# Cross attention of a decoder block: the Q and K projections as seven block products instead of eight

## The reference

```python
def _L0_xattn_ref(hidden_states, key_value_states, attention_mask, position_bias, ln_weight, w_q, w_k, w_v, w_out):
    ...
    x = _rmsnorm(hidden_states, ln_weight)
    ...
    h_q = (x @ w_q.T).reshape(b, lq, H, DH)
    h_k = (key_value_states @ w_k.T).reshape(b, lk, H, DH)
    h_v = (key_value_states @ w_v.T).reshape(b, lk, H, DH)
    score = jnp.einsum('bqhd,bkhd->bhqk', h_q, h_k)
    score = score + position_bias[None]
    m = attention_mask[:, None]
    score = jnp.where(m, score, -jnp.inf)
    score = jax.nn.softmax(score, axis=-1)
    score = jnp.where(m, score, 0.0)
    attn = jnp.einsum('bhqk,bkhd->bqhd', score, h_v).reshape(b, lq, H * DH)
    out = attn @ w_out.T
    return hidden_states + out
```

## Time and profile before

| what | us |
|---|---|
| median of 3 runs | 1096.17 |
| the profiled execution's own time | 1095.16 |
| its span, first to last instruction | 1093.1 |
| TensorE busy | 1061.4 (97%) |
| VectorE busy | 559.0 (51%) |
| ScalarE busy | 517.1 (47%) |
| GpSimd busy | 253.9 (23%) |
| one group of the cross attention, 297.47 to 350.92 | 53.45 |

### The profile page before, as it was taken

One profiled execution on the slowest core, in us unless ns is written; L12 is line 12 of the kernel. 1 busy time (PEld: TensorE's weight loads), 2 busy tenths in 40 slices (PEclk: granted clock), 3 DMA queues, 4 the chain that ended last, 5 costly groups with the idle time before them and its releaser, 6 DMA issues.

```text
span 1093.1 us, 19529 instructions
## 1 busy us (share of the span) xinstructions
PE 1061.4 (97%) x6522; PEld 920.9 (84%) x6522; DVE 559.0 (51%) x2003; ACT 517.1 (47%) x1391; POOL 253.9 (23%) x263
## 2 busy tenths in 40 slices
PE   7899988999999999999999999999999999999998
PEld 6677767888888888888888888888888888888886
DVE  6799988554434443343434343434343434343584
ACT  4889886454344344343434343434343434344412
POOL 7676665410101010101010101010101111110052
PEclk9999999999999999999999999999999999999999
DMA  4301002230202020111101010101010101000002
GB/s 151 126 21 50 2 1 69 98 131 1 82 0 82 7 74 22 59 32 49 49 32 62 19 62 19 62 19 62 19 62 19 62 19 62 19 24 1 1 1 77
DMA packets 17254, 49.59 MB, mean 45 GB/s; under 512 B 2496, under 2 KB 4928, under 8 KB 16832
## 3 DMA queue, kind: packets, MB, share of 16 engines
q1 hardware_dynamic: 16800, 45.97, 12.6%
q0 software_dynamic: 416, 3.15, 0.8%
HBM read 47.02 MB, written 2.10 MB: 45 GB/s over the span
## 4 chain that ended last, share of the span: by engine, by line
PE 83%; DVE 8%; issue 4%; POOL 2%; ACT 2%; DMA 1%; SPq 0%; POOLq 0%; DVEq 0%; ACTq 0%
PE bank L755 49%; PE bank L1571 16%; PE bank L1558 5%; PE bank L1541 5%; PE bank L1589 3%; PE bank L1548 2%; DVE sm L476 2%; POOL sm L317 1%; DVE alpha L552 1%; DMA stage<-in_wq 1%; PE bank L568 1%; PE bank L1627 1%; PE bank L681 1%; DVE mn L476 0%; ACT pr L405 0%
## 5 line engine op out<-in xcount | busy, mean ns | idle before, releaser
L938 POOL TENSOR_TENSOR bm<-mask,bias 128x512 f32<-128x512 f32 x64 | 97.2, 1520 | 709.0 <-DVE nmx L1234 455.7
L1067 ACT ACTIVATE pr<-sm,nmx 128x128 f32<-128x128 f32 x256 | 99.9, 391 | 224.3 <-DVE nmx L1234 224.3
L1246 DVE TENSOR_TENSOR at_lo<-bank,at_hi 128x512 fp32r<-128x512 f32 x64 | 44.3, 692 | 266.9 <-ACT at_hi L1081 266.7
L1252 DVE TENSOR_TENSOR acc<-acc,bank 128x512 f32<-128x512 f32 x128 | 87.7, 687 | 119.0 <-PE bank L1571 119.0
L1571 PE MATMUL bank<-wo_hi,at_hi 128*128 128x512 f32 x256 | 100.5, 392 | 0.3 <-DVE acc L1252 0.3
L1060 ACT COPY v<-bank 128x256 f32<-128x256 f32 x124 | 46.1, 372 | 115.4 <-PE bank L755 64.1
L1571 PE MATMUL bank<-wo_lo,at_hi 128*128 128x512 f32 x256 | 100.0, 391 | 0.0
L1571 PE MATMUL bank<-wo_hi,at_lo 128*128 128x512 f32 x256 | 99.9, 390 | 0.0
L755 PE MATMUL bank<-wv_hi,cT_hi 128*128 128x256 f32 x512 | 91.8, 301 | 0.2 <-DVE wv_lo L1437 0.2
L1054 ACT COPY kT<-bank 128x512 f32<-128x512 f32 x64 | 37.4, 585 | 98.4 <-PE bank L755 98.4
L755 PE MATMUL bank<-wv_hi,cT_lo 128*128 128x256 f32 x512 | 81.7, 282 | 0.0
(11 more groups left out here) (237 smaller groups left out, 2248.2 us busy)
## 6 DMA issues: line engine op xcount, KB each, us to landing
qk_raw<-in_wqk SPq DMA_DIRECT2D x32, 512.0 KB, 4.5
o_raw<-in_wo SPq DMA_DIRECT2D x16, 512.0 KB, 3.5
v_raw<-in_wv SPq DMA_DIRECT2D x15, 512.0 KB, 4.3
acc<-in_x POOLq DMA_DIRECT2D x1, 2048.0 KB, 8.1
bias<-in_bias SPq DMA_DIRECT2D x16, 128.0 KB, 3.2
out<-acc SPq DMA_DIRECT2D x8, 256.0 KB, 2.0
xT_raw<-in_xT SPq DMA_DIRECT2D x7, 256.0 KB, 2.9
stage<-in_wq SPq DMA_DIRECT2D x2, 512.0 KB, 6.9
```

Source lines behind the costliest of these rows:

```text
L938: nc.gpsimd.tensor_tensor(bm[:, s % 2], mask[:, HALF * (s // HG):HALF * (s // HG + 1), :], bias[:, s % HG:s % HG + 1, :].broadcast_to([P, ...
L1067: e = nc.scalar.activation(pr[:, s % 2, k], sm[:, s % 2, k], ACT.Exp, bias=nmx[:, s % 2, k:k + 1], accum_out=sums[:, s % 2, k:k + 1])
L1246: nc.vector.tensor_tensor(at[1][:, s // HG, s % HG], PO[:], f32(at[0][:, s // HG, s % HG]), ALU.subtract).then_inc(s_al, 1)
L1252: nc.vector.tensor_tensor(acc[:, b], acc[:, b], PX[b % 2][:], ALU.add).then_inc(s_acc, 1)
```

## The change

Groups 0 and 1 keep the eight products (`plain`). From group 2 on (`SEVEN = 2`), Q and K of a group are formed by seven block products each. Their left factors are the weight blocks A11, A12, A22 and four differences of blocks T1 to T4; their right factors are blocks of tokens (x or context) and four sums of such blocks, S1 to S4. The seven products are combined into the four output blocks by additions. In detail:

- TensorE: 7 products of 6 matmuls for Q and 7 for K replace 48 + 48 matmuls of a group. All go through the same two banks, PQ and PK, so each product waits until the one before it was taken out. They stand in a new order, spread over the steps: p5 (q, k) and p3 (q, k) in step 0, p7 in step 1, p4 and the next group's p1 in step 2, the next group's p2 and p6 in step 3.
- VectorE: 14 additions of a bank to a term in SBUF per group (`add_product`), 7 subtractions of 512 elements for low parts (`lo_op`) in place of 2 of 1024.
- ScalarE: 7 roundings of 512 elements (`hi_op`) in place of 2 of 1024, two copies of p1 in place of eight copies of Q and K.
- GpSimd: four differences of weight blocks per group (`three_turns`, `last_turn`), and seven DMAs of 1 MB per group (`load_sums`) from a DRAM tensor `block_sums` into two slots, `ring[0]` and `ring[1]`, which lie in `stage`. Seven of the eight sums (S1 to S4 for k, S2 to S4 for q) are kept in DRAM; S1 of q replaces a quarter of xnT. Slot 0 holds in turn S2q, S1k, S4k, S3k; slot 1 holds S2k, S4q, S3q. A load waits for the product that used the slot last.
- Making the sums, once, on GpSimd, between the bias masks of groups 0 and 1: 24 additions and subtractions of 128x1024 elements and 8 roundings of the same size. SyncE stores each of the seven pairs to DRAM.
- The last layer's weights, which before were loaded into `stage` in group 0, are loaded in the last group when the ring is free; splitting `wbase` moves from its step 1 to its step 2.

```diff
@@ Memory
+        self.ring = [nc.alloc_sbuf_tensor_at(f"ring{i}", [P, 2, 2, HALF * T], F32R, offset=stage_at + i * 8 * HALF * T * 2)
+                     for i in range(2)]
...
+        self.u = left(whole, "u", [P, 2, HALF * T])
@@ layer
+        SLOT_OF = {"S2q": 0, "S2k": 1, "S1k": 0, "S4q": 1, "S4k": 0, "S3q": 1, "S3k": 0}
...
+        UNITS = ("p1", "p2", "p6", "p5", "p3", "p7", "p4")
+        OPS = ("A11", "A22", "A12", "T2", "T1", "T3", "T4")
+        OP_SLOT = {"A11": "a", "A22": "c", "A12": "b", "T2": "d", "T1": "a", "T3": "b", "T4": "d"}
...
+        SUMS = ("C11", "u1", "w", "C21", "C22", "z", "C12")
+        SEVEN = 2
...
-            step(0, True, False)
-            with eng.Fori(1, NG - 1) as g:
-                step(g, False, False)
-            step(NG - 1, False, True)
+            step(0, True, False, True, True)
+            step(1, False, False, True, False)
+            with eng.Fori(SEVEN, NG - 1) as g:
+                step(g, False, False, False, False)
+            step(NG - 1, False, True, False, False)
@@ sync
+            def keep(name, hi, lo):
+                sp.wait_ge(s_ready, BLOCKS.index(name) + 1)
+                for p, ap in enumerate((hi, lo)):
+                    sp.dma_start(sums_d[BLOCKS.index(name)][:, p * 2 * HALF * T:(p + 1) * 2 * HALF * T].bitcast(F32), ap)\
+                        .then_inc(s_kept[BLOCKS.index(name) % 2], 16)
...
+            with sp.Fori(SEVEN, NG - 1) as g:
+                sp.wait_ge(s_op, done(OPS, g, "T1"))
+                load_block(g + 1, "a")
+                sp.wait_ge(s_turn, done(TURNS, g, "T4"))
+                load_block(g + 1, "c")
+                sp.wait_ge(s_wv, g + 1)
+                load_v(g + 1)
+                sp.wait_ge(s_op, done(OPS, g, "T3"))
+                load_block(g + 1, "d")
+                sp.wait_ge(s_op, done(OPS, g, "T4"))
+                load_block(g + 1, "b")
...
+            sp.wait_ge(s_unit[0], done(UNITS, NG - 1, "p7"))
+            load_experts()
@@ gpsimd
+            def load_sums(g, name, w=None, after=None):
+                k = SLOT_OF[name]
+                if after is not None:
+                    pool.wait_ge(s_unit[w], done(UNITS, g, after))
+                    nc.gpsimd.tensor_tensor(pool_gate[:, BLOCKS.index(name):BLOCKS.index(name) + 1], eps[:, 0:1], eps[:, 0:1], ALU.add)
+                nc.gpsimd.dma_start(mem.ring[k][:].rearrange("p q c n -> p (q c n)"), sums_d[BLOCKS.index(name)])\
+                    .then_inc(s_ring[k], 16)
...
+            k_differences()
             bias_mask(0, 3, True)
-            with pool.Fori(1, NG) as g:
-                for s in range(TILES):
-                    bias_mask(g, s, False)
+            k_first()
+            k_fourth()
+            k_second()
+            bias_mask(1, 0, False)
...
+            q_first()
+            q_second_split()
+            q_fourth_split()
+            q_first_split()
+            for name in BLOCKS[-2:]:
+                wait_kept(pool, name)
+            pool.wait_ge(s_s1q, 1)
+            load_sums(SEVEN, "S2q")
+            load_sums(SEVEN, "S2k")
+            three_turns(SEVEN)
+
+            def second_half(g):
+                bias_mask(g, 0, False)
+                last_turn(g)
+                bias_mask(g, 1, False)
+                load_sums(g, "S1k", 0, "p6")
+                load_sums(g, "S4q", 1, "p6")
+
+            def first_half(g):
+                bias_mask(g, 2, False)
+                load_sums(g, "S4k", 1, "p5")
+                load_sums(g, "S3q", 0, "p3")
+                load_sums(g, "S3k", 1, "p3")
+                bias_mask(g, 3, False)
@@ scalar
+            def copy_p1(g, w):
+                if isinstance(g, int) and g == SEVEN and w == 0:
+                    wait_kept(act, "S2q")
+                act.wait_ge(s_unit[w], done(UNITS, g, "p1"))
+                nc.scalar.copy(u_part[w], (PQ, PK)[w][:]).then_inc(s_copy[w], 1)
@@ vector
+            def lo_op(g, name):
...
+                nc.vector.tensor_tensor(part_of(slot, 1), block_of(qk_raw, raw), f32(part_of(slot, 0)),
+                                        ALU.subtract).then_inc(s_op, 1)
+
+            def add_product(g, w, unit, out, term):
+                dve.wait_ge(s_unit[w], done(UNITS, g, unit))
+                nc.vector.tensor_tensor(out, (PQ, PK)[w][:], term, ALU.add).then_inc(s_sum[w], 1)
...
+                if s == 2 and last:
+                    lo_base(2 * j)
+                    lo_base(2 * j + 1)
                 accumulate(n, j, (HALF + 2 * s + j) % B)
@@ tensor
+            def unit(w, slot, right):
+                pairs = [(part_of(slot, p)[:, w, c], right[q][:, c]) for p, q in PARTS for c in range(2)]
+                for i, (lhs, rhs) in enumerate(pairs):
+                    ins = nc.tensor.matmul((PQ, PK)[w][:], lhs, rhs, start=i == 0, stop=i == len(pairs) - 1)
+                ins.then_inc(s_unit[w], 1)
...
+            def product_3(g, w):
+                name = ("S4q", "S4k")[w]
+                pe.wait_ge(s_ring[SLOT_OF[name]], loaded(g, name))
+                pe.wait_ge(s_sum[w], done(SUMS, g, "w"))
+                unit(w, "c", from_ring(name))
...
-                        project_q(g if s < TILES - 1 else g + 1, (s + 1) % TILES)
-                        project_k(g if s < TILES - 1 else g + 1, (s + 1) % TILES)
+                    products_ahead(g, s, first, last, plain, plain_next)
...
                         project_v(b)
+                        if s == 1:
+                            products_between(g, s, j, last, plain, plain_next)
                         if j == 0:
-                            pv(n - 1, sp, v_ready, False)
+                            pv(n - 1, sp, head, v_ready, False)
+                        if s != 1:
+                            products_between(g, s, j, last, plain, plain_next)
...
+                    if plain and not plain_next and s == 2:
+                        product_1(g + 1, 0)
+                        product_1(g + 1, 1)
```

More of the change, by code:

```diff
@@ new lines, in load_experts @@
+                sp.dma_start(stage[:, wbase_at], a["wbase"]).then_inc(s_experts_in, 16)
+            sp.wait_ge(s_wv, 1)
+            load_v(1)
+            for i in range(HG):
+                sp.wait_ge(s_wqk[i], 1)
+                load_qk(i, 1)
+            sp.wait_ge(s_bm, TILES)
+            load_bias(1)
+            sp.wait_ge(s_wo, 1)
+            load_o(1)
+            sp.wait_ge(s_wv, 2)
+            load_v(2)
+            keep("S1k", stage[:, 0:2 * HALF * T], stage[:, 2 * HALF * T:4 * HALF * T])
@@ L1164, in step @@
+            def step(g, first, last, plain, plain_next):
+                for s in range(TILES):
+                    if first and s < 2:
+                        first_step(s)
+                    elif plain:
+                        plain_step(g, s, first, not plain_next)
+                    else:
+                        seven_step(g, s, last)
                 if last:
@@ L1470, in _, with factor, from_ring @@
         def _(pe):
+            def factor(w, chunks, half):
+                return [quarter((xnT, cT)[w][p], chunks, half) for p in range(2)]
+            def from_ring(name):
+                return [mem.ring[SLOT_OF[name]][:, p] for p in range(2)]
+            def unit(w, slot, right):
[3 more added lines that the diff above has]
+                ins.then_inc(s_unit[w], 1)
@@ L1555, in pv @@
                     pe.wait_ge(s_al, n)
[L1556 removed]
+                half = s // HG
                 for k in range(HALF):
@@ L1649, in step @@
                     had_out = not (first and s < 3)
-                    scores(n, s, first)
-                    if not (last and s == TILES - 1):
-                        project_q(g if s < TILES - 1 else g + 1, (s + 1) % TILES)
-                        project_k(g if s < TILES - 1 else g + 1, (s + 1) % TILES)
+                    head = heads_of(first or (s == 0 and plain))[sp]
+                    order = (0, 1) if s >= 2 or plain else (1, 0)
+                    scores(n, s, first, None if plain else g)
+                    products_ahead(g, s, first, last, plain, plain_next)
                     transposes(n - 1, sp)
@@ L1659, in out @@
                             pe.wait_ge(s_wo, g + 1)
-                        output((HALF + 2 * s + j) % B, 0 if s >= 2 else 1, n if j == 0 and s in (0, 2) else None)
+                        output((HALF + 2 * s + j) % B, 0 if s >= 2 else 1, order, n if j == 0 and s in (0, 2) else None)
                     if last and s in (1, 3):
```

667 lines of the change are left out of this document (518 added, 149 removed).

## The result

The changed kernel takes 1103.89 us (median of 4 runs, 1102.42 to 1104.81) beside 1096.45 for the kernel before on the same chip (4 runs). The ratio is 1.0066, 95% interval 1.0048 to 1.0083: slower by 0.7%, where 1083 us were forecast. The profiled execution took 1104.8 us, its span 1103.0.

The account below looks back on a forecast made before the run. TensorE alone was taken to bound the kernel. 1095.2 - 39.0 (matmuls) + 10 (sums) + 14 (ring loads) + 1.5 (tail) = 1081.7 us on the profiled execution, about 1083 as median; range 1060 to 1104.

Parts of the forecast that it names:

- Matmuls removed: TensorE, Q and K products: 12 fewer matmuls in each of 14 groups, 168 x 0.232 = 39.0 us saved.
- The sums, once: GpSimd's row in groups 0 and 1 ends at 293.8; TensorE stands once at p6 of group 2, 10 us.
- whether a mask would come late: GpSimd's mask of group 1, step 0 comes at 239, its scores at 243.9; no cost.
- Rival C: GpSimd and VectorE hold each other up, 3.35 us per sum: 22 us at p6, 1094.5 us; chance 0.11.
- The ring loads: Seven 1 MB loads per group, S4k for p3 of k tightest: 1.0 us waiting a group, 14 us.
- these hand-overs: Bank emptied between successive products in the loop: cost nothing; 11 us at 0.2 us a step.
- Rival B: Ring loads land after 7.5 us; p3 of k waits 2.2 us in each group: 1099.5 us; chance 0.21.
- Rival A: Ring loads come in time, landing after 4.4 us, no 14 us of waiting: 1069 us; chance 0.23.
- The tail: Last group, step 2: four VectorE subtractions for splitting `wbase` come ahead of the next masking, 1.5 us.

Follow-up runs that it names:

- e11: e8 with two tiny VectorE operations per step (negated row maxima, floored row sums) as tensor_reduce in place of tensor_scalar: 1069.48 us, ratio 0.9774 to the kernel before.
- e3: The changed kernel with GpSimd's 32 sum-making operations cut to 8 of 1024 columns each (one stays whole): 1077.31 us, ratio 0.9842 to the kernel before.
- e1: The changed kernel with VectorE's tiny experts_constants operations moved from the end of group 0 to the end of group 1: 1099.07 us, ratio 1.0028.
- e2: The changed kernel with SyncE's load of weight block d gated on k's third product, so block b behind it moves too: 1088.90 us, ratio 0.9940.
- e8: The changed kernel with e2's move, experts_constants in the last group's step 1, and the 98 ring loads issued by SyncE: 1074.40 us, ratio 0.9808.

## Why the prediction was wrong

Its sum was 1081.7 us on the profiled execution; 1104.8 came. By its own terms:

- **Matmuls removed: right.** 168 fewer, and six of a product still take 1.4 us (0.23 each). In e11, where no wait for the ring is left, a group takes 50.82 us beside 53.45 - 12 x 0.232 = 50.67.
- **The sums, once: the step that failed.** Group 2 was forecast at 297.5 + 2.8 + 10 = 310.3 and came at 321.0, 10.8 us later; 2.5 of them are the later start of this execution, 8.3 are the error of the term (18.2 in place of 10). The number alone hides how wrong it was, for the 10 us were to be one stand at p6, and there was none at p6. It was not the length of GpSimd's row either: that was priced at 2.86 for each operation with an end at 293.8, and it ended at 298.8, having begun 2.7 us later than forecast, with operations of 2.51 in the mean and after waits of 2.22, 3.15 and 1.36 us for a late VectorE and TensorE. The failure was to charge the mutual hold-up to GpSimd alone (2.38 to 2.86, "13.5 us on 24 x 2.38"), and to let TensorE keep its pace up to the first ring product. The trace had the other direction in the earlier trace rows: a tiny VectorE operation, 0.58 us where it needs 0.17, that ended with the mask. The prediction names it and scales only the other side. A row of 85 us with hardly a gap meets every `tensor_scalar` and every operation with two SBUF inputs between scores and `pv`, and each can lose one GpSimd operation, up to 2.4 us, on a path with almost no slack. e3 shows that this is the whole loss of 18.2 us, e1 that eleven tiny operations that have nothing to do with the change cost 11.4 us of it where they stood, of which 5.2 come back elsewhere in the row when they are moved away, e11 that the form of two tiny operations a step is worth 3.9 us. The prediction asked of this row only whether a mask would come late ("No cost"), and of VectorE only its busy time in a group of the loop (33.8 of 50.7 us), which can't show a hold-up.
- **Rival C** put the extra at p6 and at 3.35 us for each sum. It names a mutual hold-up, but charges it to GpSimd alone as well: 19 of the 24 sums took 2.35 to 2.42 and the longest 3.38. Its 1094.5 is about half of the way from the forecast to the result.
- **The ring loads: right in place and kind, 0.4 us too small.** The wait is at p3 of k and a DMA releases it, in every one of the 13 groups; it costs 1.38 us beside the 1.0 forecast. The landing worked out for a load alone, 5.4, was 5.1 to 5.3; blocks d and b beside it, which the prediction names, made it 6.3.
- **The rest of the loop.** With the wait forecast, a group was to take 51.67 us and took 52.21, 7.0 us over 13 groups. 0.4 of the 0.54 is the wait, as above, and e11's 50.82 has the rest: 0.15 us, spread over steps of 13.39 to 13.42 us in place of 13.36. The prediction put these hand-overs at nothing, with 11 us as the price if not; they are some 2 us, and what they are made of was not followed further. e2's step 0, 13.6 to 14.0 us, holds the small wait shown above.
- **Rival B** had the place right, a wait at p3 of k paid in each group, and its 1099.5 lies nearest to the result, by luck: it wanted landings of 7.3 to 7.5 us and 2.2 us a group. **Rival A** comes near in e2, where the loads are nearly in time: its 13 groups of the loop take 14.3 us less, against the 14 that it was worth.
- **The tail: right** within 0.6 us (94.8 us from group 15's start to the last operation, beside 98.5 - 5.6 + 1.0 + 1.5 = 95.4).
- **The end of the program: not in the sum at all,** 6.1 us. The kernel before has 2 GpSimd DMAs and its trace can't show it.

10.8 + 7.0 - 0.6 + 6.1, less 0.3 for the time outside the span, are the 23 us. Two small slips of the prediction's arithmetic change nothing: 282.3 + 13.5 is 295.8 and not 295, and rival C adds up to 1094.7.

In the trace, a VectorE operation and a GpSimd operation exclude each other for a whole instruction, whoever comes second, and the form of VectorE's operation decides whether it takes part. The Trainium skill, SBUF — State Buffer, section "Who interferes with whom", frees an operation of VectorE with one SBUF input only "outside the 2-port perf modes", and the prediction left these words out. The same section names what can use such a mode: `copy`, `cast` and `tensor_scalar` can, and `tensor_reduce` on this chip never does. e8 beside e11 agrees for `tensor_scalar` and `tensor_reduce` (2.38 and 0.16 us for the row maxima).

The Trainium skill, DMA: Bandwidth & Descriptors, section "Anatomy of one DMA — SWDGE (gpsimd) path", would have 1 MB land after 4.4 us, an estimate from its fit. Undisturbed, it was 5.1 to 5.3 on GpSimd's queue in this kernel, and the measurement decides.

## What to carry to other kernels

Before GpSimd gets a long row of elementwise work, list what VectorE has on the path to TensorE in that time, tiny operations above all: count each one that uses the shared ports as late by up to one GpSimd operation, and change its form or its place first. A load with no slack should have no other load beside it; here one later wait, which moved two other loads, was enough. And issue many loads from SyncE rather than GpSimd if its order of waits allows it. Where a wait at TensorE seems to be gone, look at its weight loads too.
